# A wait between the two row gathers that GpSimd issues for each attention head

## The reference

```python
xn = _layernorm(x, axis=-1)
x = x + _L0_attn_ref(xn, ...) + _L0_ffn_ref(xn, ...)
```

```python
out = (g1 * keep1)[:, None].astype(x.dtype) * eo[f1] + (g2 * keep2)[:, None].astype(x.dtype) * eo[f2]
```

## Time and profile before

| | us |
|---|---|
| median of 3 runs | 1812.2 |
| lowest and highest run | 1810.17 and 1918.32 |
| the profiled execution | 1807.14 |
| its span, first to last instruction | 1805.3 |
| busy in the span: PE | 1722.3 |
| busy in the span: DVE | 1486.1 |
| busy in the span: ACT | 1402.3 |
| busy in the span: POOL | 578.0 |

### The profile page before, as it was taken

One profiled execution on the slowest core, in us unless ns is written; L12 is line 12 of the kernel. 1 busy time (PEld: TensorE's weight loads), 2 busy tenths in 40 slices (PEclk: granted clock), 3 DMA queues, 4 the chain that ended last, 5 costly groups with the idle time before them and its releaser, 6 DMA issues.

```text
span 1805.3 us, 39337 instructions
## 1 busy us (share of the span) xinstructions
PE 1722.3 (95%) x15555; PEld 749.3 (42%) x15555; DVE 1486.1 (82%) x1727; ACT 1402.3 (78%) x2639; POOL 578.0 (32%) x1065
## 2 busy tenths in 40 slices
PE   6869999999999999999999999999999999999998
PEld 5437888888885222222222222222222222222226
DVE  7767777777767899898998999999999999999913
ACT  4535454445435999999999999999999999999993
POOL 1474221222200345445454454532121211112140
PEclk9989999999999999999999999999999999999999
DMA  7564233122203111111111111110101010100002
GB/s 239 197 216 148 93 108 94 59 71 88 89 12 117 35 44 36 49 34 40 45 37 48 35 41 43 38 41 23 32 23 32 23 29 27 27 11 5 5 1 94
DMA packets 92280, 109.66 MB, mean 61 GB/s; under 512 B 17472, under 2 KB 67264, under 8 KB 92096
## 3 DMA queue, kind: packets, MB, share of 16 engines
q1 hardware_dynamic: 85952, 90.36, 16.0%
q0 software_dynamic: 6144, 16.79, 3.2%
HBM read 72.77 MB, written 33.82 MB: 59 GB/s over the span
## 4 chain that ended last, share of the span: by engine, by line
PE 66%; ACT 27%; POOL 3%; DVE 2%; issue 1%; DMA 1%; ACTq 0%; SPq 0%; DVEq 0%; POOLq 0%
ACT arena_t L780 25%; PE banks L1223 18%; PE banks L1211 12%; PE banks L1262 10%; PE banks L1242 10%; PE banks L1193 8%; POOL arena_v L558 2%; PE banks L1282 2%; ACT o_raw L759 2%; PE banks L1116 2%; PE banks L1344 2%; PE banks L1162 1%; PE banks L1127 0%; DMA arena_x<-x_in 0%; DVE row_half L993 0%
## 5 line engine op out<-in xcount | busy, mean ns | idle before, releaser
L993 DVE TENSOR_REDUCE row_half<-banks 128x2 f32<-128x1024 f32 x1024 | 1189.7, 1218 | 144.7 <-PE banks L1193 136.5
L780 ACT ACTIVATE arena_t<-banks 128x512 f32<-128x512 f32 x2048 | 1085.2, 600 | 57.7 <-PE banks L1211 30.9
L1223 PE MATMUL banks<-arena_t,v_ring 128*17 128x256 f32 x8192 | 643.6, 386 | 26.2 <-ACT o_raw L759 26.1
L1223 PEld LDWEIGHTS banks<-arena_t,v_ring 128*17 128x17 f32 x8192 | 136.2, 95 | 403.4 <-issue 244.2
L1211 PE MATMUL banks<-arena_q 50*128 50x512 bf16 x960 | 286.2, 383 | 0.6 <-ACT arena_t L780 0.3
L1211 PE MATMUL banks<-qk_ring 50*128 50x512 bf16 x896 | 267.1, 387 | 7.1 <-ACT arena_t L780 4.1
L1193 PE MATMUL banks<-arena_q 48*128 48x512 bf16 x960 | 268.4, 384 | 0.5 <-DVE row_half L993 0.2
L1193 PE MATMUL banks<-qk_ring 48*128 48x512 bf16 x896 | 249.1, 382 | 1.1 <-DVEq L986 1.0
L744 ACT ACTIVATE arena_t<-banks 128x512 f32<-128x512 f32 x128 | 76.5, 598 | 205.8 <-PE banks L1242 197.1
L1262 PE MATMUL banks<-w_parts,hidden_parts 128*128 128x256 f32 x1536 | 196.3, 286 | 0.0
L1262 PEld LDWEIGHTS banks<-w_parts,hidden_parts 128*128 128x128 f32 x1536 | 187.1, 192 | 13.6 <-issue 13.6
(11 more groups left out here) (147 smaller groups left out, 1355.0 us busy)
## 6 DMA issues: line engine op xcount, KB each, us to landing
expert_rows<-arena_r SPq DMA_DIRECT2D x16, 512.0 KB, 3.0
q_stack<-arena_q SPq DMA_DIRECT2D x8, 768.0 KB, 4.9
k_stack<-arena_q SPq DMA_DIRECT2D x8, 768.0 KB, 3.5
v_heads<-arena_v SPq DMA_DIRECT2D x4, 1088.0 KB, 5.6
v_ring<-v_heads SPq DMA_DIRECT2D x64, 68.0 KB, 3.0
arena_x<-x_in SPq DMA_DIRECT2D x4, 1024.0 KB, 6.3
token_rows<-arena_x SPq DMA_DIRECT2D x4, 1024.0 KB, 7.8
arena_v<-w_gate_in SPq DMA_DIRECT2D x4, 1024.0 KB, 6.7
```

What stands on the lines that cost most here:

```text
L780: nc.scalar.activation(probs[:, kt % PSLOTS, q, :], banks[:, ST_BANKS[ring_place(i) % 3], :], ACT.Exp).then_inc(exp_done, 1)
L993: nc.vector.tensor_reduce(halves[:, :, j // 2], banks[:, SMAX_PAIRS[m % 2]:SMAX_PAIRS[m % 2] + 2, :], AX.X, ALU.max, negate=True).then_inc ...
L1223: mm = pe.matmul(banks[QUAD * q:QUAD * q + VP, OT_BANK, columns], v_ring[:, g % SLOTS, kt, :], probs[:, kt % PSLOTS, q, columns], start=(k ...
```

## The change

Between the first and the second indirect DMA of `gather(t)`, POOL now waits until the first one's rows have landed. The semaphore of the slot stands at 32 for each earlier tile of that slot, so the value waited for is 32 * (t // 2) + 16.

```diff
                 for c in range(2):
+                    if c == 1:
+                        pool.wait_ge(gather_in[t % 2], 32 * (t // 2) + 16)
                     nc.gpsimd.indirect_dma_start(
                         out=gathered[:, t % 2, c, :], out_offset=None, in_=expert_rows,
                         in_offset=bass.IndirectOffsetOnAxis(ap=slot_i[:, c, t:t + 1], axis=0)).then_inc(gather_in[t % 2], 16)
```

## The result

The changed kernel took 1796.2 us (median of 5 runs, 1791.9 to 1798.1) against 1812.2 us; the ratio to before is 0.9912, with an interval of 0.9896 to 0.9929. It is faster by 0.9%, or 16 us, where I forecast no change worth the name. In the profiled executions the span fell from 1805.3 to 1794.2 us, by 11.1 us. One execution of the kernel before took 1918.3 us, in a slower state of the chip, and is left out of the ratio.

A forecast was written before the change was run, and what follows sets the result against it. PE and ACT together were taken to bound the attention steps, with DVE close behind. About 2 us of DVE stands, the gathers' 13 us unchanged, made 1812.2 + 2 = 1814 us; range 1799 to 1830.

The forecast's parts named there:

- The wait's length: POOL, between the gathers: second issue 4.0 us after the first instead of 1.36; some 85 us new idleness.
- Hidden from the next head: POOL before `scale_heads`: the 2.6 us delay fits in 7.83 us of idleness before the reciprocal, so costs nothing.
- The splits: POOL's splits queued behind gathers come 2.6 us later; DVE's turn stands 1.0 and 0.8 us in two heads, about 2 us.
- the recorded margins: Time to spare between split parts ready and DVE's turn: 1.6, 1.8, 2.65 and 3.6 us in the tightest heads.
- What the gathers cost the others: Heads with gathers: 0.42 us longer each, 13 us in all, seen as ACT waiting for PE; forecast left it unchanged.
- the faster rival: Making descriptors while the same queue's packets move holds ACT; the wait removes it: -13 + 2 = -11, 1801 us; chance 0.24.
- The slower rival: Each gather starting on an empty queue disturbs ACT once, the second now too: +13 + 2 = +15, 1827 us; chance 0.24.
- the long landing: First gather's semaphore comes only 9.4 us after issue, DVE stands some 36 us: from 1848 us upward; chance 0.03.

The follow-up runs named there:

- e3_single: Kernel before with only the first gather of each tile issued, the second expert's share left out: 1792.7 us, ratio 0.9896.
- c3_bias_between: Kernel before with the bias addition moved between the two gathers, 1.98 us apart, no wait: 1793.5 us, ratio 0.9909.
- e1_fill1: Kernel before with one POOL memset between the two gathers instead of a wait for rows, issues 2.3 us apart: 1793.5 us, ratio 0.9905.

## Why the prediction was wrong

*The wait's length: right.* I put the second issue at 4.0 us after the first; it came at 4.08 in the row above, and the landings had a median of 3.7 us (2.8 to 4.5). The new idleness of POOL was forecast near 90 us and measured at 92.5. The estimate from the Trainium skill, "DMA: Bandwidth & Descriptors", section "Anatomy of one DMA — SWDGE (gpsimd) path", 2.3 us, was under the shortest of these landings.

*Hidden from the next head: right.* POOL's wait before the reciprocal went from 7.83 to 6.12 us at the place shown, where I had put 5.2. The reciprocal itself came 1.0 us later after the first issue than before, and DVE's stand of 1.37 us lies ahead of it. Nothing waited for `scale_heads`.

*The splits: right in kind, too small.* I had 2 us in two heads, from 2.6 us of delay; it was 4.0 us in four. The four heads were those of the earlier trace rows. The second issue came 4.00 to 4.24 us after the first in them, and each stand is 0.3 to 1.2 us longer than that delay and the recorded margins give, so the margins had shrunk as well; why, no run shows.

*What the gathers cost the others: the step that failed.* I wrote that I take this term "as a price of having a gather's pair at all, paid once", and left 13 us where they were. The runs show that it is no price of a pair but of a close pair: one gather costs nothing (e3_single), and two cost nothing from 1.98 us apart (c3_bias_between). I had 2 us of stands added to an unchanged 13 us; in fact the 32 heads with gathers lost 11.1 us, with 4.0 us of stands in it. The rows on which I could have seen it stood in the trace: all pieces that I had read came behind the second issue, and none behind the first. I used this for the faster rival, and gave it 0.24.

*The faster rival: right in size, wrong in its reason.* It took the making of descriptors beside moving packets for the cause. e1_fill1 has just that and no longer heads. That its price, -13 + 2 = -11, equals the 11.1 us of the span is in part luck, since its 2 us of stands were 4.0. Its 1801 us missed the measured 1796.2 by 5, and all of that is in the step from one profiled execution to the median: it was 5.1 us in the kernel before and 0.2 us in the kernel after (1796.0 and 1796.2).

*The slower rival and the long landing* are refuted by e3_single and by the landings. The rule of the Trainium skill, "SBUF — State Buffer", section "Who interferes with whom", that only the port pair of VectorE and GpSimd causes contention, would have had nothing change. What the prediction made of it did not come true, by ACT's wait of 13.1 against 2.5 us; whether the disturbance is contention for SBUF at all, no run shows. What exactly holds the handovers up stays open. Three things are shown: in this kernel it needs two indirect DMAs issued less than about 2 us apart (there at 1.66, gone at 1.98), it is no smaller at half their bytes, and of the five chips on record three showed it and two did not.

The range ended at 1799 and the time is 1796.2. It took in the faster rival's centre, but left only 2 us below it, though I had myself read the price from one execution with 5 us between it and the median.

## What to carry to other kernels

Two indirect DMAs that GpSimd issues back to back can slow the handovers between the other engines (here by 0.3 to 0.5 us in a step of 18.3), though GpSimd itself is idle for half of a step; read this from the pieces of waiting that follow the second issue, and from the length of a step with and without the pair. Put work that GpSimd has anyway between the two: moving the bias addition there gave 1793.5 us against 1796.4 for the wait on the same chip, and cost nothing on chips without the effect. A wait does the same by its distance alone, and then adds what stands behind it on the queue. And compare on more than one chip: here the kernel before differed by 1% between them, as much as the whole change.

## What the runs showed of the hardware

The kernel before took 1810.2 to 1813.1 us (medians) on the chips with the disturbance and 1793.9 and 1794.4 on the two without; all versions with two gathers 1.98 us or more apart took 1793.5 to 1797.6 on any of them. The heads without gathers agree everywhere, at 18.32 us, and the mean granted clock is 1.00 in both stretches of the kernels before and after, so it is no matter of a slower clock. No execution of the kernel before fell between the two groups: with the disturbance its executions took 1806.2 us or more, without it 1796.1 or less. But each of the five chips on record was used at one time only, so that the chip decides, and not something else that differed between those times, is likely and not shown. Whether the changed kernel is slower than before on a chip without the disturbance, by the 4 us or so of DVE's stands, was not tried: it never ran on one. Where between 1.66 and 1.98 us the edge lies is open as well.
